# A 7x7 convolution on one core: from two 128x64 column halves with a shifted copy to four 64x64 tiles that share one copy

## What is computed

```python
kern = construct_kernel(weight, P)              # (32, 32, 7, 7), bilinear scatter of 9 points
conv = conv2d(groupnorm_per_channel(x), kern, padding=3) + bias
out = x + conv
```

## Time and profile before

| | |
|---|---|
| median of 3 runs (lowest, highest) | 335.46 us (334.76, 336.88) |
| the profiled execution: time, span in the profile | 337.36 us, 335.5 us |
| busy share of the span: PE, DVE, ACT, POOL | 90%, 84%, 62%, 46% |
| share of the 16 DMA engines: loads and stores by hardware queues, `xb<-xs` by POOL's queue | 40.3%, 38.3% |
| instructions | 9554 |

### The profile page before, as it was taken

How to read it: one execution, slowest core, us unless ns; L and a number is a source line. 1 busy time by engine, 2 the same in 40 slices (tenths; PEclk the granted TensorE clock), 3 DMA queues, 4 the chain that set the end, 5 groups by cost and what they waited for, 6 DMA issues and landing times.

```text
span 335.5 us, 9554 instructions
## 1 busy us (share of the span) xinstructions
PE 302.6 (90%) x3380; PEld 205.9 (61%) x3380; DVE 280.3 (84%) x420; ACT 209.6 (62%) x327; POOL 153.7 (46%) x259
## 2 busy tenths in 40 slices
PE   4920599999999999999999999999999999999990
PEld 2710366666566676766666666666666666666660
DVE  4379698999889898989799898999898989897231
ACT  2268796855867685957676867777776856451200
POOL 6422535454362828273535455463728282644000
PEclk9675599999999999999999999999999999999998
DMA  8942355979899898979898999999898949398604
GB/s 143 151 95 72 106 136 128 246 175 239 195 208 230 172 245 195 239 160 259 186 233 190 236 205 235 195 215 235 202 226 170 259 115 228 98 225 227 142 2 96
DMA packets 128253, 61.37 MB, mean 183 GB/s; under 512 B 122068, under 2 KB 122068, under 8 KB 128228
## 3 DMA queue, kind: packets, MB, share of 16 engines
q1 hardware_dynamic: 115204, 24.90, 40.3%
q0 software_dynamic: 9312, 35.34, 38.3%
q10 hardware_dynamic: 3712, 0.80, 1.3%
HBM read 12.88 MB, written 12.85 MB: 77 GB/s over the span
## 4 chain that ended last, share of the span: by engine, by line
PE 71%; issue 8%; DVE 7%; DMA 5%; POOL 4%; ACT 2%; DVEq 0%; POOLq 0%; ACTq 0%
PE ps_s L792 23%; PE ps_x L792 18%; PE ps_eo L792 14%; PE ps_y L792 13%; DMA xb<-xs 4%; DVE e L451 3%; POOL xn L693 2%; POOL xb L681 2%; PE ps_eo L761 1%; PE ps_x L761 1%; DMA wnat<-L_conv_weight 1%; DVE xs L470 1%; DVE d L451 1%; ACT xs L343 1%; PE ps_stat L730 1%
## 5 line engine op out<-in xcount | busy, mean ns | idle before, releaser
L681 POOL DMA_DIRECT2D xb<-xs x192 | 93.5, 494 | 82.4 <-DVE xs L470 81.9
L792 PE MATMUL ps_s<-xb,w 128*64 128x392 f16 (+1 forms) x576 | 107.8, 338 | 0.8 <-DMA xb<-xs 0.7
L792 PE MATMUL ps_s<-xs,w 128*64 128x392 f16 (+1 forms) x576 | 108.3, 338 | 0.0
L693 POOL TENSOR_SCALAR xn<-xraw,scale,offset 32x784 f32<-32x784 f32 x32 | 51.3, 1607 | 70.4 <-DVE offset L448 70.4
L792 PEld LDWEIGHTS ps_s<-xs,w 128*64 128x64 f16 x576 | 63.9, 112 | 21.5
L792 PE MATMUL ps_x<-xb,w 128*64 128x392 f16 x384 | 70.9, 341 | 0.0
L792 PE MATMUL ps_x<-xs,w 128*64 128x392 f16 x384 | 70.9, 341 | 0.1
L792 PEld LDWEIGHTS ps_s<-xb,w 128*64 128x64 f16 x576 | 63.9, 112 | 10.8 <-DMA xb<-xs 1.9
L792 PE MATMUL ps_eo<-xb,w 128*64 128x392 f16 (+1 forms) x384 | 69.1, 337 | 0.0
L792 PE MATMUL ps_eo<-xs,w 128*64 128x392 f16 (+1 forms) x384 | 69.1, 337 | 0.0
L343 ACT ACTIVATE xs<-e 128x900 f16<-128x900 f32 x48 | 45.6, 950 | 24.8 <-DVE e L451 15.1
(11 more groups left out here) (90 smaller groups left out, 415.7 us busy)
## 6 DMA issues: line engine op xcount, KB each, us to landing
xb<-xs POOLq DMA_DIRECT2D x96, 180.0 KB, 4.1
xb<-xs POOLq DMA_DIRECT2D x96, 179.0 KB, 4.3
xraw<-x SPq DMA_DIRECT2D x124, 98.0 KB, 2.9
out<-result SPq DMA_DIRECT2D x124, 98.0 KB, 5.0
xraw<-x ACTq DMA_DIRECT2D x4, 98.0 KB, 3.9
out<-result ACTq DMA_DIRECT2D x4, 98.0 KB, 3.6
wnat<-L_conv_weight POOLq DMA_DIRECT2D x1, 36.0 KB, 3.8
pts<-L_conv_P POOLq DMA_DIRECT2D x2, 1.1 KB, 3.0
```

The source lines that it names most:

```text
L681: pool.dma_start(dst[32 * g:32 * g + 32, 0:run - QP * past], src[32 * f:32 * f + 32, QP * past:run]).then_inc(shifted[par][b], DMA)
L693: pool.tensor_scalar(xn[96:128, u % 2, SLOTS * m:SLOTS * m + ROWS, PAD:PAD + SIDE], image(u % RING, m)[96:128, :].rearrange("p (n w) -> p ...
L792: last = pe.matmul(into[p:p + HALF, :, :, 0:wide], w[:, n // 2, s, q, t, :], xs_or_xb[:, par, s, n % 2, :, t:t + ROWS, q:q + wide], start= ...
```

## The change

- The array is used as four tiles of 64 rows by 64 columns. Each of the 102 products of a unit is now two pairs: one over partitions 0 to 63 ("upper", `product(0, ...)`) and one over 64 to 127 ("lower", `product(HALF, ...)`), each pair into both column halves. The lower pair of product c is issued behind the upper pair of product c + 14 (`LAG = 14`, in `step`), across the border between units too. A stream counts as done (`conv_done`) with its last lower product. Before a stream's first lower product PE waits for its own last upper one (`upper_done`). Waits sit on added `nop` instructions.
- Both column halves read `xs`: for one of them the slot is shifted by one row for the upper partitions. `xb`, `shift` and their semaphores go. The other half needs the filters with partitions 0 to 63 and 64 to 127 exchanged: `wx`, filled by two DMAs of SP at the start, for which PE waits before the first product.
- `WINDOW` and the loading order of row phases change, so `xraw` no longer lies in the order of the output. The image is loaded a second time, in output order, into `photo`, by 8 DMAs per unit that POOL issues (`image_again`), and `seed` reads `photo`. SP's loads now wait for `normalised` in place of `seeded`.
- Layouts: `xs` rows hold the two images interleaved (`[..., QS, PER]`, 30 fp16 a row), so an offset `q = 1` is 4 bytes; 28 (or 26) fp16 run on end. `xn` is kept as odd and even columns apart, so that reads which stepped by 4 fp32 step by 2, and reads that stepped by 2 step by 1 (of the image) or 2 (of `d`, as before). `high` and `low` write with a step of two fp16. `seed` writes, and `outs_2` and `outs_4` read, PSUM with images interleaved; these two are split into one DVE instruction per image (`OUTS = 7`).
- The fold of the statistics is split into an upper part at stream 4 and a lower part three products later.
- DVE's and ACT's order within a step is not touched.

```diff
-WINDOW = (2, 1, 0, 3)
+WINDOW = (0, 1, 2, 3)
+
+LAG = 14
...
         def fetch(queue, u, r, m, g):
             queue.dma_start(image(r, m)[32 * g:32 * g + 32, :].rearrange("c (n w) -> c n w", w=SIDE),
-                            dram_rows(x, u, m, g)).then_inc(x_loaded[r], DMA)
+                            dram_rows(x, u, m, (2 - g) % GROUPS)).then_inc(x_loaded[r], DMA)
...
         def halves(par, n, s, count):
-            wide = width(s) if count == 1 else QS
-            return xs[:, par, s:s + count, n, :, :, 0:wide].rearrange(
-                "p s m n q -> p (s m n) q" if count == 1 else "p s m n q -> p s (m n) q", s=count)
+            if count == 1:
+                return xs[:, par, s, n, 0:SLOTS, 0:width(s)].rearrange("p n q m -> p m n q")
+            return xs[:, par, s:s + count, n, 0:SLOTS].rearrange("p s n q m -> p s m (n q)")
...
+            sp.wait_ge(wlo_ready, FILTER_STEPS)
+            for a in (0, HALF):
+                sp.dma_start(wx[a:a + HALF].rearrange("p n s a b c -> p (n s a b c)"),
+                             w[HALF - a:2 * HALF - a].rearrange("p n s a b c -> p (n s a b c)")
+                             ).then_inc(filters_exchanged, DMA)
             with sp.Fori(0, UNITS // RING - 1) as it:
                 for h in range(RING):
                     u = it * RING + h
-                    sp.wait_ge(seeded, 2 * u + 2)
+                    sp.wait_ge(normalised, NORMS * u + NORMS)
                     sp.wait_ge(last_group_normalised, NORMS * u + NORMS)
                     load(u + RING, h)
...
-            def seed(u, r, k, first=False):
+            def seed(u, par, k, nth, first=False):
 
                 if first:
                     act.wait_ge(marked, k + 1)
                 else:
-                    act.wait_ge(combined, OUTS * (u - 1) + (3, 5)[k])
-                photo = xraw[:, PER * r:PER * (r + 1), :].rearrange("p m n -> p (m n)")
-                act.activation(pair_of((ps_x, ps_y)[k]), two_phases(photo, k),
+                    act.wait_ge(combined, OUTS * (u - 1) + (4, 7)[k])
+                act.wait_ge(photo_loaded[par], LOAD * (nth + 1))
+                act.activation(pair_of((ps_x, ps_y)[k]).rearrange("p (n m) k -> p m n k", m=PER),
+                               photo[:, par].rearrange("p m (n k) -> p m n k", k=4)[:, :, :, k::2],
                                ACT.Copy, scale=scales[:, 2:3]).then_inc(seeded, 1)
 
-            def step(u, h, nth, nxt, stats, early, first=False, second=False):
...
-                less(e[:, 1, :, :, 0:QS], xn[:, par, :, 1:4 * QS + 1:4], 4, xn[:, par, :, 3:4 * QS:4])
+                less(e[:, 1], xn[:, par, 0, :, 0:2 * QS:2], 2, xn[:, par, 0, :, 1:2 * QS:2])
...
-                add(two_phases(result[:, par, :], 0), pair_of(ps_x), part[:, 0])
+                for m in range(PER):
+                    add(two_phases(result[:, par, PLANE * m:PLANE * (m + 1)], 0), pair_of(ps_x)[:, m::PER],
+                        part[:, 0, m::PER])
...
-                less(d[:, :, :, 0:half], xn[:, par, :, 0:2 * half:2], 2, xn[:, par, :, 1:2 * half:2])
+                even = xn[:, par, 1, :, 0:half]
+                before = bass.AP(tensor=even.tensor, offset=even.offset - 1, ap=even.ap)
+                less(d[:, :, :, 0:half], before, 1, xn[:, par, 0, :, 0:half])
...
             def outs_4(u, par):
                 dve.wait_ge(conv_done, NS * u + 9)
-                dve.wait_ge(combined, OUTS * u + 4)
-                add(two_phases(result[:, par, :], 1), pair_of(ps_y), part[:, 1])
+                dve.wait_ge(combined, OUTS * u + 5)
+                for m in range(PER):
+                    add(two_phases(result[:, par, PLANE * m:PLANE * (m + 1)], 1), pair_of(ps_y)[:, m::PER],
+                        part[:, 1, m::PER])
...
+            def image_again(u):
+
+                if u > 1:
+                    pool.wait_ge(seeded, 2 * (u - 1))
+                for m in range(PER):
+                    for g in range(GROUPS):
+                        pool.dma_start(photo[32 * g:32 * g + 32, u % 2, m, :].rearrange("c (n w) -> c n w", w=SIDE),
+                                       dram_rows(x, u, m, g)).then_inc(photo_loaded[u % 2], DMA)
...
             normalise(0)
+            image_again(0)
+            normalise(1)
+            image_again(1)
+            for u in range(2, UNITS):
+                normalise(u)
+                image_again(u)
...
+            PRODUCTS = [(s, n, q, t) for s in range(NS) for n in range(3) for q in range(2 if s < NS - 1 else 1)
+                        for t in range(2)]
+            FIRST = [[p[0] for p in PRODUCTS].index(s) for s in range(NS)]
+            LAST = [f - 1 for f in FIRST[1:]] + [len(PRODUCTS) - 1]
+            def product(p0, par, c):
+                s, n, q, t = PRODUCTS[c]
+                into = bank(s).rearrange("p (n q) -> p n q", n=ROWS)
+                wide = min(QW, width(s) - q)
+                for p, filt, slot in ((HALF, w, t), (0, wx, t + (p0 == 0))):
+                    last = pe.matmul(into[p:p + HALF, :, 0:PER * wide], filt[p0:p0 + HALF, n // 2, s, q, t, :],
+                                     xs[p0:p0 + HALF, par, s, n % 2, slot:slot + ROWS, q:q + wide, :].rearrange(
+                                         "p n q m -> p n (q m)"),
+                                     start=p0 == 0 and c == FIRST[s] and s not in (4, 5, 7, 8),
+                                     stop=p0 != 0 and c == LAST[s], skip_group_check=True)
+                if c == LAST[s]:
+                    last.then_inc(conv_done if p0 else upper_done, 1)
+            def lower(u, par, c):
+                if c in FIRST:
+                    pe.wait_ge(upper_done, NS * u + FIRST.index(c) + 1)
+                    pe.nop(nofuse=True)
+                product(HALF, par, c)
+            def step(u, par, stats, early, first=False):
+                for c, (s, n, q, t) in enumerate(PRODUCTS):
+                    if c == FIRST[s]:
+                        if s == 0 and not first:
+                            pe.wait_ge(combined, OUTS * (u - 1) + 5)
+                        if s == 3:
+                            pe.wait_ge(m11_ready, u + 1)
+                        if s == 4:
+                            if stats:
+                                pe.wait_ge(ssq_ready, u + 3)
+                                pe.wait_ge(var_ready, u + 2)
+                                if early:
+                                    pe.wait_ge(sum_ready, u + 4)
+                                    pe.wait_ge(negmean_ready, u + 3)
+                                pe.nop(nofuse=True)
+                                fold_part(0, 0, 2 * PER if early else PER)
+                            pe.wait_ge(seeded, 2 * u + 1)
+                        if s == 6:
+                            pe.wait_ge(combined, OUTS * u + 2)
+                        if s == 7:
+                            pe.wait_ge(seeded, 2 * u + 2)
+                        pe.wait_ge(lo_ready, NS * u + s + 1)
+                        pe.nop(nofuse=True)
+                    if stats and c == FIRST[4] + 3:
+                        pe.wait_ge(upper_folded, u + 1)
+                        pe.nop(nofuse=True)
+                        fold_part(HALF, 0, 2 * PER if early else PER)
+                    product(0, par, c)
+                    if c >= LAG:
+                        lower(u, par, c - LAG)
+                    elif not first:
+                        lower(u - 1, 1 - par, c - LAG + len(PRODUCTS))
+            pe.wait_ge(filters_exchanged, 2 * DMA)
             for u in range(2):
-                step(u, u, 0, True, True, first=u == 0)
```

More of the change, by code:

```diff
@@ L40 @@
 LOAD = PER * GROUPS * DMA
-SHIFTS = GROUPS * DMA
 CHUNKS = 3
@@ L127, in build @@
         bias_loaded = sem("bias_loaded")
-        shifted = [[sem(f"shifted_{'even' if par == 0 else 'odd'}_{b}") for b in range(THIRDS)] for par in range(2)]
+        photo_loaded = [sem("photo_loaded_even"), sem("photo_loaded_odd")]
+        filters_exchanged = sem("filters_exchanged")
         sum_ready = sem("sum_ready")
@@ L370, in step @@
                 middle(u, first)
-                seed(u, h, 0, first)
+                seed(u, h % 2, 0, half, first)
                 if early:
@@ L376, in step @@
                         high(u + 1, a, *batch, first=first)
-                seed(u, h, 1, first)
+                seed(u, h % 2, 1, half, first)
                 if stats:
@@ L776, in _ @@
             both_moments(1)
-            def convolve(u, par, s, nth):
-                i, j = STREAMS[s]
-                pe.wait_ge(whi_ready, FILTER_OF[s])
-                pe.wait_ge(lo_ready, NS * u + s + 1)
-                into = bank(s).rearrange("p (m n q) -> p m n q", m=PER, q=QW)
-                order = [(n, q, t) for n in range(3) for q in range(2 if s < NS - 1 else 1) for t in range(2)]
-                fresh = s not in (4, 5, 7, 8)
-                for c, (n, q, t) in enumerate(order):
-                    if n == 2 and order[c - 1][0] == 1:
```

(32 more changed lines are left out.)

88 lines of the change are left out of this document (35 added, 53 removed).

## The result

The changed kernel takes **377.83 us** (median of 4 runs, 376.17 to 378.00) against 335.11 us (334.64 to 336.88), 1.125 times the time before, 95% interval 1.120 to 1.131. The forecast was 358 us. Direction and mechanism held; the loss is about twice the forecast's.

The account below looks back on a forecast made before the run. PE's products were taken to bound the kernel before, 17.72 us a unit. Span 335.5 + 3.3 (start) + 16.4 (units) + 1.6 (end) + 1.0 (late loads) = 357.8; 359.7 with what lies around, 1.9 above median: 358 us, range 348 to 386.

Parts of the forecast that it names:

- the forecast's own case: Whole kernel: VectorE and PE wait for each other through the lag, 358 us, 348 to 370; chance 0.68.
- Rival 1: `outs_2` and `outs_4`: strided PSUM reads 1.7 times as slow, +1.1 us per unit, 374 us; chance 0.10.
- Rival 3: POOL's issuing of the second load becomes the bound: issues of 2.2 us, 386 us or more; chance 0.06.
- Direction, ring: Unit border: VectorE waits 2.6 us or more for lagged products, PE 1.5 to 2.3 for `outs_3`; slower by over 1%: 0.93.
- Products: TensorE's products: aligned reads at 0.167 us, or 0.155 for 13 columns, 16.8 us a unit, 0.9 less.
- Rivals 2 and 5: TensorE: 2, weight loads take turns, 0.22 us a product, 422 us (0.06); 5, reads still at 0.191, 365 us (0.04).
- Strided PSUM reads: VectorE's `outs_2` and `outs_4`, read per image: nothing taken for the stride; upper bound 1.7-fold.
- GpSimd the bound: POOL: 8 issues of 1.05 us plus normalising, 11.8 of 19.2 us, hidden; POOL the bound above 1.98 an issue.
- The steady unit: Unit period: 18.8 us from VectorE alone, 19.2 with ScalarE's statistics, 18.7 in steps without statistics.
- The lag counts twice: Lower products 14 products (2.3 us) late: `outs_4` starts at T+2.6, and `outs_2` can start 14 products later, at 15.9.
- Start: Before the first product: `wx` delays it to 41.3 from 37.33; unit 1 begins 3.3 us later (2 to 6).
- Late loads, 2.6 us: SP's loads no longer wait for the seeds: of 3.6 us of late-load waits 2.6 go, 1.0 stays.

Follow-up runs that it names:

- Experiment 4: The changed kernel with VectorE making the odd and plain differences of unit u+2 ahead of `outs_4` of unit u: 355.91 us, ratio 1.057.
- experiment 7: The changed kernel with the second image load issued by SyncE, one unit ahead, instead of by GpSimd: 380.01 us (one run).
- Experiment 6: The changed kernel with GpSimd's normalising cut from unit 2 on to one column pair a row instead of 28: 369.98 us (one run).
- experiment 2: The changed kernel with `LAG` 18 instead of 14: 404.24 us (one run), 22.1 us a unit.
- Experiment 8: The changed kernel with 20 products of zeros on TensorE ahead of the wait for the exchanged filters: 377.47 us.
- experiment 1: The kernel before with the new layouts alone, two column halves and the copy `xb` kept: 330.29 us, ratio to before 0.981.

## Why the prediction was right, and where it was too small

The way the kernel moved and the reason given for it are right. That 377.8 lies inside the range of 348 to 386 is partly luck: the forecast's own case went from 348 to 370, and the part above it was there for rivals 1 and 3, neither of which came about. The time got there by a steady unit 1.44 us longer than the sum and a start 3.4 us later.

- *Direction, ring.* Right. `outs_4` starts at T+2.65 (2.6 foreseen), VectorE's gap is 2.9 and TensorE's 1.7 (foreseen: 2.6 or more, 1.5 to 2.3), a smaller one stands at stream 3 and 0.3 at the statistics. Experiment 4 closes VectorE's gap, and with it the waits behind the late `odd_differences`, and returns 22 of the 42.7 us: about half of the loss was this order. Steps without statistics: 18.7 foreseen, 18.85 measured; the last: -0.85 foreseen, -0.90 measured.
- *Products.* Right: 0.167 and 0.155, equal at both offsets. Rivals 2 and 5 fall.
- *Strided PSUM reads.* Right at nothing: the pair of halves takes 1.08 us from start to start (184.05 to 185.13), as foreseen. Rival 1 falls.
- *GpSimd the bound.* False: 0.64 us an issue (1.05 foreseen), and POOL busy for 35%. Rival 3 falls by experiment 7 too.
- *The steady unit: 19.2 foreseen, 20.64 measured.* This is the term that was sized wrong; it makes up nearly all of the 15 us by which the stretch between the first and the last `outs_4` exceeds the sum, out of 18 in the whole. Followed along T = 167.48, the start of stream 0: `outs_4` and `odd_differences` are on time (T+4.81). The `high` pass takes 1.10 us from start to start, not 0.86 (the fp16 halves are now written with a step of two; its mean went from 950 to 1227 ns in the groups of ScalarE, and is 1233 with the layouts alone), `m11` is complete only with the record's end of `middle`, 0.66 after its start where the sum had 0.56, and the fold waits 0.31 and takes its own time: stream 4 starts at T+9.78, not 9.2. `outs_1` was "done by 12.9" and taken to start at 11.7 without a wait; it waits 0.52 for stream 3's lower half, which ends only 14 products into the late stream 4, and starts at 12.5. Then the `low` passes: 1.19 instead of 1.09, 0.68 instead of 0.6, the same strided writes, +0.25. So `outs_2` starts at 16.57, not 15.9, and does not wait. The last `low` was put at 1.01 and takes 1.74 from start to start: +0.73. Sum 0.67 + 0.04 (the rounding of `outs_3` to 17.95) + 0.73 = 1.44. Experiment 6 takes back 0.6 of the 0.73; the rest of the 1.44 is read from the trace, not tried by itself.
- *The lag counts twice.* The sum did pass it twice, at `outs_4` and at `outs_2`; experiment 2's 0.37 a product (two would be 0.33) bears the number out. The place was wrong: in the trace the second one is `outs_1`, which the sum let start without a wait.
- *GpSimd beside VectorE* was priced at nothing. The earlier trace rows showed the sign of it: `normalise` there took 3.38 us; after the change the same two take 2.61 (183.33 to 185.94), ending 1.04 before the end of VectorE's long pass. Before, GpSimd's pair was the longer one and VectorE's passes beside it kept 0.60 and 1.09; after the change it is the other way round. The Trainium skill (SBUF — State Buffer, Who interferes with whom) states that an instruction of VectorE with two SBUF inputs contends with a GpSimd instruction that reads SBUF, and that issue order decides who blocks; the 1.19 and 3.56 against 1.88 and 2.62 of experiment 4 agree.
- *Start: 5.6 foreseen with the lag, 9.0 measured.* The two `wx` transfers land in 5.9 us and cost 1.2 to issue: first product 42.44, not 41.3. Missed was the clock: it stays at half until about 49.5, while before it was full from 42 on the earlier trace rows, the engine having been at work since 37.33. Experiment 8 prices that at 4.2 us (4.65 less the 0.44 of its earlier first product).
- *Late loads, 2.6 us.* Right as to these: units of the changed kernel mostly vary by 0.1 us in the middle. The same loads hold up experiment 1.

## What to carry to other kernels

A lag between two halves of a result is paid at each place where a consumer must free what the producer needs next; count these places, and give the waiting engine other work before it commits to the wait. When instructions are shifted in time, look at who meets whom: a two-input VectorE pass beside which GpSimd's pass used to stretch may be the one that is stretched now. Try the parts of a combined change by themselves: here the layouts win about 5 us and the rest of the change loses 47; with the order rewritten it still loses 16.

## What the runs showed of the hardware that was not expected

- Four 64x64 tiles take 0.165 us for a product of 392 columns into each, no more than two 128x64 halves (0.167), weight loads included. With the lag equal to the 12 products of a stream, the first lower product of a stream came 0.31 to 0.33 us after the product ahead of it.
- A moving operand of 392 columns in runs of fp16 that begin on word boundaries costs 0.167 us where the runs of 14 that begin on half a word cost 0.19.
- GpSimd's normalising (1.31 us each) and a VectorE subtraction of two SBUF tiles hold each other up: where they met, either VectorE's pass took 1.85 to 1.88 us instead of 1.19, or GpSimd's pair 3.56 instead of 2.62.
- The half granted clock at the start of the changed kernel cost about 4.2 us, and zeros on idle TensorE remove it. In both kernels with four tiles and zeros a standstill of TensorE of 3.9 and 4.4 us in mid-run, beside nine more transfers of the instruction queue, took that back, though no instruction of the loop had changed; a lag of 12 without zeros had such a standstill too (5.1 us), at an unchanged number of instructions.
